# An LSTM over 512 steps: forget gate first, the bias inside the input weights, logits for four steps at once, running sums behind the turn of the state

## The reference

```
xn = layernorm(x)                                  # over the 256 features
x_proj = xn @ W_ih.T + b_ih + b_hh                 # 4 gates x 256
def step((h, c), xp):                              # 512 times, one after the other
    i, f, g, o = split(xp + h @ W_hh.T, 4)
    c = sigmoid(f) * c + sigmoid(i) * tanh(g)
    h = sigmoid(o) * tanh(c)
    return (h, c), h
logits = hs @ W_lin.T + b_lin                      # 2 per position; the larger one picks
```

## Time and profile before

| | us |
|---|---|
| three runs | 4398.80, 4400.19, 4393.27 (median 4398.8) |
| the profiled execution | 4399.52 |
| its span, first to last instruction | 4397.4 |

### The profile page before, as it was taken

One profiled execution on the slowest core, in us unless ns is written; L12 is line 12 of the kernel. 1 busy time (PEld: TensorE's weight loads), 2 busy tenths in 40 slices (PEclk: granted clock), 3 DMA queues, 4 the chain that ended last, 5 costly groups with the idle time before them and its releaser, 6 DMA issues. The chain is left out here.

```text
span 4397.4 us, 143561 instructions
## 1 busy us (share of the span) xinstructions
PE 3990.7 (91%) x55713; PEld 2861.6 (65%) x55713; DVE 3495.9 (79%) x9566; ACT 2881.3 (66%) x7050; POOL 1190.6 (27%) x1028
## 2 busy tenths in 40 slices
PE   8999999996999999999998999978888888888882
PEld 5666666653665666666665777767777777777772
DVE  7999999986889889889887888846666666666666
ACT  7999999986888888888885777733333333333330
POOL 4777777771222222222221011100000000000000
PEclk9999999998999999999999999999999999999996
DMA  2222221211000000000002434411111111111115
GB/s 67 80 90 60 78 78 59 78 55 35 30 21 30 30 22 28 30 23 27 30 19 87 143 125 135 146 37 37 38 42 41 39 38 41 40 40 40 40 37 168
DMA packets 327039, 251.03 MB, mean 57 GB/s; under 512 B 172888, under 2 KB 291032, under 8 KB 324312
## 3 DMA queue, kind: packets, MB, share of 16 engines
q1 hardware_dynamic: 324824, 233.40, 18.5%
q10 hardware_dynamic: 1536, 8.39, 0.6%
HBM read 157.27 MB, written 67.12 MB: 51 GB/s over the span
## 5 line engine op out<-in xcount | busy, mean ns | idle before, releaser
L2630 PE MATMUL lstm_G_psum<-next_Whh,lstm_HT 128*32 128x192 f32 x8192 | 440.2, 333 | 238.2 <-DVE lstm_HT L2762 238.1
L2701 ACT ACTIVATE lstm_TC<-lstm_G_psum 128x192 f32<-128x192 f32 x512 | 169.6, 331 | 658.1 <-PE lstm_G_psum L2630 658.1
L1615 ACT ACTIVATE ssm_EX<-ssm_Z_psum,ssm_tok 128x256 f32<-128x256 f32 (+1 forms) x1024 | 371.8, 423 | 156.0 <-PE ssm_Z_psum L1446 86.2
L2622 PE MATMUL lstm_G_psum<-next_Wih,lstm_XT 128*32 128x192 f32 x8192 | 428.1, 327 | 0.0
L2630 PEld LDWEIGHTS lstm_G_psum<-next_Whh,lstm_HT 128*32 128x32 f32 x8192 | 214.1, 109 | 321.2 <-DVE lstm_HT L2762 287.5
L2749 DVE SCALAR_TENSOR_TENSOR lstm_AB<-lstm_TC 128x128 f32<-128x128 f32 x512 | 149.6, 292 | 311.6 <-ACT lstm_TC L2701 309.5
L647 ACT ACTIVATE g_PR<-g_S,g_nmax 128x512 f32<-128x512 f32 x512 | 367.9, 722 | 4.8 <-DVE g_nmax L784 4.8
L791 DVE COPY g_PT<-g_PT_psum 128x512 f32<-128x512 f32 x512 | 344.1, 683 | 26.3 <-PE g_PT_psum L514 21.8
L638 ACT ACTIVATE g_relu<-g_Z_psum,g_src 128x512 f32<-128x512 f32 x512 | 346.0, 682 | 20.8 <-PE g_Z_psum L507 20.6
L2924 POOL TENSOR_SCALAR lstm_rstd<-lstm_mv 128x4 f32<-128x4 f32 x32 | 7.2, 226 | 1278.7 <-DVE lstm_mv L2743 1278.7
L784 DVE CUSTOM_DVE_ANT_0 g_S<-g_Z_psum,g_relu 128x512 f32<-128x512 f32 x512 | 345.0, 683 | 10.1 <-ACT g_relu L638 8.6
(11 more groups left out here) (311 smaller groups left out, 10921.5 us busy)
## 6 DMA issues: line engine op xcount, KB each, us to landing
g_ADJ<-in_adj SPq DMA_DIRECT2D x64, 1024.0 KB, 7.1
x<-g_XO SPq DMA_DIRECT2D x64, 512.0 KB, 5.3
g_X<-in_x SPq DMA_DIRECT2D x32, 512.0 KB, 4.3
ssm_X<-x SPq DMA_DIRECT2D x32, 512.0 KB, 3.9
x<-ssm_OUT SPq DMA_DIRECT2D x32, 512.0 KB, 2.9
g_X<-x SPq DMA_DIRECT2D x32, 512.0 KB, 4.4
lstm_U<-x SPq DMA_DIRECT2D x128, 128.0 KB, 3.5
lstm_V<-lstm_U SPq DMA_DIRECT2D x128, 128.0 KB, 3.2
```

Of the source, the lines that this page charges most:

```text
L1615: ins = act.activation(EX[h % NE][:, col:col + n], Zb[c][:, i * CHUNK:i * CHUNK + n], ACT.Exp, bias=tok[b.slot][:, i, c, h:h + 1])
L2622: pe.matmul(bank[32 * j:32 * (j + 1), 0:n], XT[c.slot][:, kc, :, t], Wih[:, kc, j, first:last], start=False, stop=False, skip_group_check= ...
L2630: ins = pe.matmul(bank[32 * j:32 * (j + 1), 0:last - first], HT[t % 2][:, 32 * kc:32 * (kc + 1)], Whh[:, kc, j, first:last], start=False, ...
L2701: act.activation(TC[t % 2][:, 0:3, :].rearrange("p g e -> p (g e)"), Gb[t % 2][:, 0:IFG], ACT.Tanh).then_inc(s["tg"], 1)
```

## The change

- **Forget gate first, a shared bank.** `hidden` becomes three parts: `forget_hidden` (64 columns) into the first half of bank `FO`, `input_hidden` (gates i and g, 128 columns) into bank `IG`, and `output_hidden` (64 columns) into the second half of `FO`, which first waits until ACT has read the forget half. ACT makes three gate activations (`TF`, `IG`, `TO`), DVE two products (`KP` = (1+f) c, `IN` = (1+i) g) of 64 columns, then the cell state `C`.
- **Bias inside the input weights.** POOL adds 1 to the shift, so x arrives as xn + 1; each row of `W_ih` gets (b - its sum)/256 added (`fold_bias`, in four stages behind sequences 15 to 18 of the attention phase). The bias matmuls of `inputs`, the bf16 rows and their transfers go. `inputs` writes 128 + 128 columns.
- **Logits for four steps at once.** `HT` keeps all 16 steps of a chunk; `logits` takes four steps as one weight of 128 columns, after steps t = 0, 4, 8, 12.
- **Order beside the steps.** On DVE `norm` now stands ahead of `beside`, `own` starts at t = 0, and `counted` is shared out anew; ACT normalises at t = 10 and 11 and copies out at 13 and 14; PE turns x at 12 and 13.

```diff
+            def fold_bias(stage):
+
+                if stage == 0:
+                    v.wait_ge(s["nat"], 16 * 9)
+                    v.wait_ge(s["small"], 16 * (4 + 8 + 16))
+                    v.tensor_reduce(wsum[:, :], nat_ih[:, :, :], AX, ALU.add).then_inc(s["bsum"], 1)
+                    v.tensor_tensor(bsum[:, :], bparts[:, 0, :], bparts[:, 1, :], ALU.add).then_inc(s["bsum"], 1)
+                if stage == 1:
+                    v.wait_ge(s["bsum"], 2)
+                    v.tensor_tensor(bsum[:, :], bsum[:, :], wsum[:, :], ALU.subtract).then_inc(s["bsum"], 1)
+                    v.wait_ge(s["bsum"], 3)
+                    v.tensor_scalar(bsum[:, :], bsum[:, :], 1.0 / D, None, ALU.mult).then_inc(s["bsum"], 1)
+                if stage == 2:
+                    v.wait_ge(s["bsum"], 4)
+                    v.tensor_tensor(nat_ih[:, :, :], nat_ih[:, :, :], bcast(bsum[:, :], D), ALU.add
+                                    ).then_inc(s["folded"], 1)
...
-                if k == 15:
-                    next_bias()
+                if 15 <= k < 19:
+                    fold_bias(k - 15)
...
+                for bank, pair, read in ((FOb[t % 2], 1, s["to"]), (IGb[t % 2], 0, s["tg"])):
                     c.wait(pe, read, S, t - 1)
-                    n = last - first
...
+                            pe.matmul(bank[32 * j:32 * (j + 1), 0:2 * HB].rearrange("p (a e) -> p a e", a=2),
+                                      XT[c.slot][:, kc, :, t],
+                                      Wih[:, kc, j, :].rearrange("p (a b e) -> p a b e", a=2, b=2)[:, :, pair, :],
+                                      start=(kc == 0), stop=False, skip_group_check=True)
...
+            def forget_hidden(c, t):
                 for kc in range(KC):
-                    ins = pe.matmul(LGb[c.slot][0:B, 2 * t:2 * t + 2], turned_h[:, 32 * kc:32 * (kc + 1)], wl[:, kc, :],
+                    c.wait(pe, s["ht"], KC * S, KC * t + kc + 1)
+                    for j in range(J):
+                        ins = pe.matmul(FOb[t % 2][32 * j:32 * (j + 1), 0:HB], turned_state(c, t, kc),
+                                        Whh[:, kc, j, HB:2 * HB], start=False, stop=(kc == KC - 1), skip_group_check=True)
+                ins.then_inc(s["gf"], 1)
+
+            def input_hidden(c, t):
+                for kc in range(KC):
+                    for j in range(J):
+                        ins = pe.matmul(IGb[t % 2][32 * j:32 * (j + 1), 0:2 * HB].rearrange("p (a e) -> p a e", a=2),
+                                        turned_state(c, t, kc),
+                                        Whh[:, kc, j, :].rearrange("p (a b e) -> p a b e", a=2, b=2)[:, :, 0, :],
+                                        start=False, stop=(kc == KC - 1), skip_group_check=True)
+                ins.then_inc(s["g"], 1)
+
+            def output_hidden(c, t):
+                c.wait(pe, s["tf"], S, t + 1)
+                for kc in range(KC):
+                    for j in range(J):
+                        ins = pe.matmul(FOb[t % 2][32 * j:32 * (j + 1), HB:2 * HB], turned_state(c, t, kc),
+                                        Whh[:, kc, j, 3 * HB:4 * HB], start=False, stop=(kc == KC - 1),
+                                        skip_group_check=True)
+                ins.then_inc(s["go"], 1)
+
+            def logits(c, g):
+
+                for kc in range(KC):
+                    ins = pe.matmul(LGb[c.slot][:, 2 * g:2 * g + 2],
+                                    HT[c.slot][:, kc, GR * g:GR * (g + 1), :].rearrange("p t b -> p (t b)"), wl[:, kc, :],
...
+                if g == GR - 1:
+                    ins.then_inc(s["lgp"], 1)
...
-                    hidden(c, t)
+                    forget_hidden(c, t)
+                    input_hidden(c, t)
+                    output_hidden(c, t)
...
-                    if t > 0:
-                        logit(c, t - 1, HT[t % 2])
-                    elif prev:
-                        logit(c + -1, S - 1, HT[0])
+                    if t > 0 and t % GR == 0:
+                        logits(c, t // GR - 1)
+                    elif t == 0 and prev:
+                        logits(c + -1, GR - 1)
...
-                    if nxt and t in (11, 12):
-                        turned(c + 1, t - 11)
+                    if nxt and t in (12, 13):
+                        turned(c + 1, t - 12)
...
+                c.wait(act, s["gf"], S, t + 1)
+                c.wait(act, s["keep"], S, t - 1)
+                act.activation(TF[t % 2][:, :], FOb[t % 2][:, 0:HB], ACT.Tanh).then_inc(s["tf"], 1)
                 c.wait(act, s["g"], S, t + 1)
-                c.wait(act, s["ab"], S, t - 1)
-                act.activation(TC[t % 2][:, 0:3, :].rearrange("p g e -> p (g e)"), Gb[t % 2][:, 0:IFG], ACT.Tanh
+                c.wait(act, s["inp"], S, t - 1)
...
-                    if nxt and t in (8, 9):
-                        normalised(c + 1, 2 * (t - 8))
-                        normalised(c + 1, 2 * (t - 8) + 1)
-                    if nxt and t in (12, 13):
-                        evacuate(c + 1, t - 12)
+                    if nxt and t in (10, 11):
+                        normalised(c + 1, 2 * (t - 10))
+                        normalised(c + 1, 2 * (t - 10) + 1)
+                    if nxt and t in (13, 14):
+                        evacuate(c + 1, t - 13)
...
             def step(c, t):
+                c.wait(v, s["tf"], S, t + 1)
+                c.wait(v, s["c2"], S, t)
+                v.scalar_tensor_tensor(out=KP[:, :], in0=TF[t % 2][:, :], scalar=1.0, in1=C[:, :], op0=ALU.add,
+                                       op1=ALU.mult).then_inc(s["keep"], 1)
                 c.wait(v, s["tg"], S, t + 1)
-                c.wait(v, s["c2"], S, t)
-                v.scalar_tensor_tensor(out=AB[:, :, :], in0=TC[t % 2][:, 0:2, :], scalar=1.0, in1=TC[t % 2][:, 2:4, :],
-                                       op0=ALU.add, op1=ALU.mult).then_inc(s["ab"], 1)
-                c.wait(v, s["ab"], S, t + 1)
-                v.scalar_tensor_tensor(out=TC[(t + 1) % 2][:, 3, :], in0=AB[:, 1, :], scalar=0.5, in1=AB[:, 0, :],
-                                       op0=ALU.mult, op1=ALU.add).then_inc(s["c2"], 1)
+                v.scalar_tensor_tensor(out=IN[:, :], in0=IG[t % 2][:, 0, :], scalar=1.0, in1=IG[t % 2][:, 1, :],
+                                       op0=ALU.add, op1=ALU.mult).then_inc(s["inp"], 1)
+                c.wait(v, s["inp"], S, t + 1)
+                c.wait(v, s["keep"], S, t + 1)
+                v.scalar_tensor_tensor(out=C[:, :], in0=KP[:, :], scalar=0.5, in1=IN[:, :], op0=ALU.mult, op1=ALU.add
+                                       ).then_inc(s["c2"], 1)
...
-                c.wait(v, s["lgp"], S, t - 1)
+                if t == 0:
+                    c.wait(v, s["lgp"], 1, -1)
                 for kc in range(KC):
-                    part_of = slice(32 * kc, 32 * (kc + 1))
-                    v.transpose(HT[(t + 1) % 2][:, part_of], H[c.slot][:, t, part_of]).then_inc(s["ht"], 1)
+                    v.transpose(HT[c.slot][:, kc, t, :], H[c.slot][:, t, 32 * kc:32 * (kc + 1)]).then_inc(s["ht"], 1)
...
+                v.tensor_tensor(flag[:, :], lg[:, :, 1], lg[:, :, 0], ALU.is_gt).then_inc(s["flag"], 1)
+                c.wait(v, s["flag"], 1, 1)
...
+            BESIDE = {3: (0, 1), 4: (2, 3), 5: (4, 5), 6: (6, 7), 7: (8, 9, 10), 8: (11,), 9: (12,), 10: (13,), 11: (14, 15)}
...
+                if t == 0:
+                    own(c, 0)
...
+                for k in BESIDE.get(t, ()):
+                    counted(c, k)
+                if t in (8, 12):
+                    before_it(c, t // 4 - 2)
+                if t in (9, 13):
+                    before_added(c, t // 4 - 2)
+                if t in (10, 14):
+                    up_to_it(c, t // 4 - 2)
+                if t in (11, 15):
+                    up_to_taken(c, t // 4 - 2)
...
                     step(c, t)
+                    if nxt and 3 <= t < 3 + TILES + 1:
+                        norm(c + 1, t - 3)
                     if prev:
                         beside(c + -1, t)
-                    if nxt and 3 <= t < 3 + TILES + 1:
-                        norm(c + 1, t - 3)
...
-                g.tensor_scalar(shift[:, :], shift[:, :], -1.0, None, ALU.mult).then_inc(s["shift"], 1)
+                g.tensor_scalar(shift[:, :], shift[:, :], -1.0, 1.0, ALU.mult, ALU.add).then_inc(s["shift"], 1)
```

More of the change, by code:

```diff
@@ L2598, in _ @@
         def _(pe):
-            pe.wait_ge(s["setup_v"], 1)
+            pe.wait_ge(s["setup_v"], 2)
             def turned(c, kc):
@@ L2612, in inputs @@
                     c.wait(pe, s["xt"], KC, KC)
-                for bank, first, last, read in ((Gb[t % 2], 0, IFG, s["tg"]), (Ob[t % 2], IFG, 4 * HB, s["to"])):
+                for bank, pair, read in ((FOb[t % 2], 1, s["to"]), (IGb[t % 2], 0, s["tg"])):
                     c.wait(pe, read, S, t - 1)
-                    n = last - first
-                    for j in range(J):
```

(7 more changed lines are left out.)

162 lines of the change are left out of this document (51 added, 111 removed).

## The result

The changed kernel takes **4356.5 us** (median of 4 runs, 4352.8 to 4365.5) against 4399.5 (4 runs beside them, 4393.3 to 4401.4): ratio **0.991**, 95% interval 0.989 to 0.993. The forecast was 4334, its range 4308 to 4380. The direction is right and the time lies inside the range, but of the 65 us of gain forecast a third, 22 us, didn't come, and the time lies outside the forecast's own range of 4312 to 4352, nearer to the rivals at 4360 and 4364. Only the traces can say which of them it is. The profiled execution took 4352.8, the fastest of the four; its span is 4351.0 us against 4397.4.

A forecast was written before the change was run, and what follows sets the result against it. The prediction took each step to be bound by a ring of waits of 2.68 us, with no engine full. From 4399.5, the terms -56 - 24.5 + 5 + 7 + 3 gave 4334 us, range 4308 to 4380.

The forecast's parts named there:

- ring: Chain from one step's hidden matmuls to the next's, setting the step time: 2.68 to 2.57 us, 507 x 0.11 = -56 us.
- rows late: Rival: raw rows come late in most chunks, need 1.2 us above the room, +30 us, 4364; chance 0.14.
- wait for the shift: ACT's wait for POOL at t = 8 goes with normalisation at t = 10 and 11: 31 x 0.79 = -24.5 us.
- logits and turn at t = 12: PE's four-step logits and the turn of x together overrun the step: 31 x 0.17 = +5 us (0 to +12).
- raw rows later: SP's next load starts later, room 20.8 against need 20.6 us; half the chunks slightly late: +7 us (0 to +40).
- removed bias matmuls: Dropping the steps' bias matmuls on PE counts as nothing; they pay for the new wait of output_hidden.
- bias in the attention: fold_bias's two passes make PE lose about 2.1 us each in the attention phase: +3 us (-1.5 to +5).
- 1.88 + 0.44 + 0.54 = 2.86 against 2.57 ... I take 0.2: PE at t = 12: inputs end, logits, turn of x against step length; 0.28 late, from 0 to 0.40, taken as 0.2.
- a longer ring heals it: Argument against raw rows coming late in most chunks: longer steps give the loads more room, by eight steps.
- DVE late: Rival: without instruction overlap, DVE's full steps t = 1, 7, 11 run late, 0.85 us a chunk, +26, 4360; chance 0.13.
- Weight-load-bound pieces: Rival: forget-piece rounds take the weight load's 0.14 us instead of 0.055, +117 us, 4507; chance 0.07.
- A sign of being wrong that came: Among the listed signs of a wrong forecast: a granted clock below 1.00 in the steps.

The follow-up runs named there:

- run 6: Changed kernel with IN computed over 128 columns instead of 64, C taking one half of it: 4378.1 us, ratio 0.995 to the kernel before.
- run 7: Changed kernel with input and cell gates ahead of the forget gate on PE, ACT and DVE, widths and banks kept: 4423.0 us, ratio 1.005 to the kernel before.
- run 5: Kernel before with only the normalisation moved to t = 10 and 11, turn and copies one step later: 4378.2 us, ratio 0.995.
- run 3: Changed kernel with the normalisation at t = 8 and 9 and the logits group of t = 12 at t = 14: 4322.7 us, ratio 0.983.
- run 1: Changed kernel with the normalisation back at t = 8 and 9: 4336.0 us, ratio 0.986 to the kernel before.
- run 8: Kernel before without the bias matmuls of the steps, bias left out of the gates: 4395.5 us against 4399.2, ratio 0.9990.
- run 9: Changed kernel, normalisation at t = 8 and 9, turn at 10 and 11, copies at 11 and 12, fold_bias passes cut to 8 elements: 4321.8 us; uncut 4324.0.
- run 2: Changed kernel with only the logits group of t = 12 moved to t = 14: 4356.5 us, ratio 0.991 to the kernel before.

## Why the prediction was right, and where its sizes were off

The mechanism of the ring was right, and so was the largest term. Two terms were too small, by 8 and 13.5 us: the median came out 22 us late, the profiled execution 19. The range held only because it was wide enough for the rival "rows late", whose cause this is in part.

| term | predicted | measured | shown by |
|---|---|---|---|
| ring | -56 | -56 | both traces; runs 6 and 7 |
| wait for the shift | -24.5 | -23 | both traces; run 5 (-21) |
| logits and turn at t = 12 | +5 | +13 | both traces; run 3 (13 to 15) |
| raw rows later | +7 | +20.5, of which some 19 at the rows | both traces; run 1 (17 to 20) |
| removed bias matmuls | 0 | -2 (held within the t = 12 row) | run 8 |
| bias in the attention | +3 | +3 | both traces; run 9's time is too coarse |
| outside, code unchanged | 0 | -4 | not explained; in the traces of the runs the first step ends anywhere from 2912 to 2921 us |

**Ring.** 2.58 against 2.57. Of 0.109, run 6 puts 0.07 on DVE's product (64 columns for 128). The rest fits the narrower tanh (0.28 for 0.33 us) less the 0.01 allowed for the third piece; that part is read from the traces, not tried. Nor was the new place of the norm ahead of the running sums, which the sum for the raw rows counts as 0.48 of room less. The order forget first buys nothing up to C. It is needed nonetheless: in run 7 the shared bank makes the output gate late.

**The wait for the shift.** The number was right, the reason only for the old gates. In the kernel before, the move is worth 21 us (run 5). In the changed kernel the wait costs nothing with the normalisation at t = 8 and 9 either (run 1: 0 us over the median at t = 9). So the 23 us would have come without the move, which the prediction paid for with 7 us and the kernel with 20.

**The turn.** The step that failed is "1.88 + 0.44 + 0.54 = 2.86 against 2.57 ... I take 0.2". Measured, the three are 2.02 + 0.47 + 0.56 = 3.05. The inputs began 1.02 behind the first matmul (2996.71), about as forecast, and their first four rounds took 0.44, as forecast (to 2997.15). From there to the logits it was 0.56, not 0.44. These 0.12 of the 0.19 are what the sum put at nothing: the gap in front of the logits' first weight load, shown above. The logits and the turn add 0.03 and 0.02. And I cut a sum of 0.28 to 0.2, though nothing in the rows asked for it. Where PE has no slack, each such hundredth goes into the ring. The 0.46 is beyond even the bound of 0.40, since this bound moved the price of the logits alone.

**Raw rows.** The step that failed is the estimate that half of the chunks would be late "by a third of" one slow issue. Room and need were close: 20.66 measured, 20.8 forecast. The need was 20.6, taken from chunk 0, where the last landing was 1.5 behind the last issue. In the changed kernel DVE waited in 18 of the 30 later chunks, the need went up to 23.1 (over 1 us of waiting in 9 of them), and the norm began 1.2 to 3.5 behind the last issue. A need taken from the one chunk that showed it was a lower edge, not a middle. This is the rival "rows late" at half its size (it had +30 more; 13 more came). What made single chunks slow isn't settled. The sentence "a longer ring heals it" was right, and runs 5, 6 and 7 show it; its reverse I did not draw: whatever shortens the steps between a load's start and its need takes away the room, so the gains of the other edits were partly paid for here. Run 2 is that in pure form.

**Rivals.** DVE late: refuted, the steps t = 1, 7 and 11 are at their middle within 0.003 us of the median of all. The instructions overlap as before (2985.33 + 0.34 = 2985.67, and the next starts at 2985.59). The Trainium skill, "VectorE: DVE Perf Modes", section The DRAIN you can't avoid, read as every instruction waiting for an empty pipe, would have made it 26 us; these rows don't bear that reading out for instructions that wait for nothing. Weight-load-bound pieces: refuted, the forget piece takes 2985.62 - 2985.37 = 0.25 for four rounds, 0.06 each, where the rival needed 0.09.

**A sign of being wrong that came.** The granted clock in the steps was 0.99, not 1.00. In the steps it fell to 1.2 GHz three times for a few us, in chunks 0, 1 and 20, each time behind a wait for raw rows of over 2 us (last section).

## What to carry to other kernels

A ring of waits costs its widths and its handovers: 64 columns less in one DVE instruction on it were 36 us over 512 steps, and 144 us more work for ACT beside it didn't show in the steps. Before crediting a shorter step, list each transfer that has a fixed number of steps to arrive: its room shrinks with every step won, and its need must be taken from its slow cases. Move a waiting operation only after asking whether the wait still reaches the ring; here the rest of the change had already made it free, and the move spent 5 us of the loads' room for nothing.
